# Moving the value products of a pair of query tiles behind the next scores and two sets of transposes, in the last batch and in the first batch's first two groups

## The chip, the cores and the metric

The kernel runs on one core of a Trainium2 chip, as a single launch. The metric is the time of the whole program in microseconds (us) on the device: 785.86 us for the kernel before, the median of three runs (783.3 to 787.12). A core has five engines that run their own instruction lists in order and meet at semaphores: TensorE (PE in the profile, for matrix products and for transposes through an identity matrix), VectorE (DVE), ScalarE (ACT), GpSimd (POOL) and SyncE (SP, which issues transfers).

## The reference, cut to what matters

The reference is one decoder layer on 4 batches of 512 tokens with 512 features: attention, then an expert layer, then a feed-forward layer with quantized weights. The change lies in the attention alone, which has 16 heads of 32 features, a band of keys and four sink keys:

```python
q = q.reshape(b, s, NUM_HEADS, HEAD_DIM).transpose(0, 2, 1, 3)
...
scores = jnp.einsum('bhqd,bhkd->bhqk', q, k) * scale
...
    banned = _sliding_window_banned(s, kv_len)       # (j >= SINKS) & (j < pos - WINDOW)
    scores = jnp.where(banned[None, None], -jnp.inf, scores)
probs = jax.nn.softmax(scores, axis=-1)
out = jnp.einsum('bhqk,bhkd->bhqd', probs, v)
out = out.transpose(0, 2, 1, 3).reshape(b, s, D_MODEL)
return out @ Wo.T + bo
```

A query keeps the four sink keys, all keys after it, and the 128 keys before it. Scores and projections are formed as three products of rounded halves (high by high, high by low, low by high), so that they keep nearly full precision.

## The kernel before

The attention phase takes the first 457 us of the profiled execution. It works batch by batch (`b`), in each batch by groups of four heads (`g`), and in each group by four tiles of 128 queries (`qt`). One step of this is a **unit** (g, qt). `g = 4` of a batch stands for group 0 of the next one, since the work is staged one batch ahead.

What PE does in a unit is written out by hand in `unit` of `tensor_program` and sets the order of everything: first the **scores** of the next unit (L948, and the band's mask at L956), into the PSUM tile `s_ps`; then the transposes of this unit's probabilities, slots 0 and 1 (L976, four heads each, into the two halves of `pT_ps`); then one **side** product into `side_ps` if the tables `PROJECTED` and `IN_ROUND` have one for this unit (a projection Q, K, V or O of twelve products, L889); then the slots 2 and 3. In units with qt = 2 a slot holds the sinks (L972), in those with qt = 3 slots 2 and 3 hold the sinks and the reciprocal sums `norm` (L969). At the end of the units with an odd qt comes `attend_pair`: the **value products** of the two query tiles qt - 1 and qt (L998, and L990 for the sinks) into `pv_ps`. In the first three batches the units (1, 3), (2, 0), (2, 1) and (2, 2) close with a transposition of the next batch's input, **X0** to X3 (L894), also through `side_ps`.

Round this loop three engines hand work on. DVE takes the maxima of the scores (L724), copies slots 1 and 3 out of PSUM (L745; L742 for the reciprocal sums), and multiplies the finished values with the reciprocal sums (`attn_of`, L736). ACT copies slots 0 and 2 (L560) and takes the **exponentials** of the next unit's scores (`exps`, L548), which it writes to `probs`. The next scores wait until all four exponentials of the unit before have read `s_ps`. `side_ps` is one bank: each side product waits until the one before it has been taken away, a projection K by ACT (`k_hi`, L523 and L525) and then DVE (`k_lo`, L644 and L648).

The exponentials of query tiles 0 and 1 and of tiles 2 and 3 share room: `probs` holds the pair 0, 1 in its first part and the pair 2, 3 in a part that overlaps tile 1. So the exponentials of tile 3 write where those of tile 1 were, and those of the next group's tile 1 where those of tile 3 were.

Groups 0 and 1 of the first batch and groups 1 to 3 of the last have few side products or none: `PROJECTED` names Q and K for group 1, V for group 2, and the last batch has no next one to prepare. There is also a chain of small DVE steps that routes tokens to experts; it stands between the units of the first batch (`tiles_needed` and its fellows). GpSimd (`widen`, `split`, L404 to L415) widens the reciprocal sums and splits the finished values.

Of the kernel before, what the change touches and what calls it, by code (L numbers as in the profile page):

```python
# [11 lines left out]
BATCH, SEQ, D = 4, 512, 512  # L12
# [3 lines left out]
HG = HEADS // GH  # L16
# [21 lines left out]
ROUTE_COUNTED, ROUTE_STEPS, ROUTE_DENSE = 10, 34, 42  # L38
# [21 lines left out]
def attention_phase(nc, io, x1, x2, slot_tokens, dense_tokens, sh):  # L60
# [7 lines left out]
    with ExitStack() as ctx:  # L68
# [123 lines left out]
        def width(qt):  # L192
            sink, kts, _ = blocks(qt)
            return SINKS * sink + P * len(kts)
# [21 lines left out]
        def units_before(b, g, qt):  # L216
            return b * GU + g * TT + qt
# [29 lines left out]
        def projected(b, g, qt):  # L247
            name = PROJECTED[g].split()[qt]
            return None if name == "-" or (g and not taken(b, name)) else name
# [9 lines left out]

        def in_key_order(keys):  # L260
            return keys.rearrange("p (u n) -> p u n", u=2)[:, :, SINKS:]

        def key_columns(keys, rows, g, qt):
            if qt < 2:
# [238 lines left out]
        def scalar_program(act):  # L503
# [39 lines left out]

            def exps(b, g, qt, s):
                act.wait_ge(max_ready, units_before(b, g, qt) * 2 + s + 1)
                at = BAND - width(qt) if qt >= 2 else 0
                for h in (2 * s, 2 * s + 1):
                    nc.scalar.activation(weights[qt][:, h, at:at + width(qt)], s_ps[:, h, 0:width(qt)], ACT.Exp,  # L548
                                         bias=neg_max[:, qt % 2, h:h + 1],
                                         accum_out=sums[:, g % 2, qt, h:h + 1]).then_inc(exp_done, 1)  # L550
# [57 lines left out]
        def vector_program(dve):  # L608
# [54 lines left out]
            done = [0]  # L663
# [68 lines left out]

            def attn_of(b, g):
                dve.wait_ge(slot_copied[1], copies_before(b, g, TT - 1, SLOTS - 1) + 1)
                dve.wait_ge(heads_done, b * HG + g + 1)
                nc.vector.tensor_tensor(norm[:], pv_ps[:], norm[:], ALU.mult).then_inc(attn_ready, 1)  # L736

            def copy_slot(b, g, qt, k):
# [9 lines left out]
            def unit(b, g, qt, last):  # L748
# [11 lines left out]
                if more:  # L760
                    maxima(b, *nxt, 0)
                    maxima(b, *nxt, 1)
                if qt == 0 and 0 < g < HG:
                    attn_of(b, g - 1)
                if prepare and qt in (1, 2):
                    for t in (2 * qt - 2, 2 * qt - 1):
# [1 line left out]
                if qt >= 2:  # L768
                    a, z = columns(qt, "sink")
                    dve.wait_ge(exp_done, units_before(b, g, qt) * GH + GH)  # L770
                    nc.vector.tensor_reduce(sinks[:], weights[qt][:, :, a:z].unsqueeze(3), AX.X, ALU.max).then_inc(sinks_gathered, 1)
                copy_slot(b, g, qt, 1)
                if prepare and qt in (1, 2):
                    dve.wait_ge(stats_step, coming * TT + 2 * qt)
                    for t in (2 * qt - 2, 2 * qt - 1):
                        variance_of(coming, t)
# [74 lines left out]
            weight_lo(5)  # L851
            for t in (1, 2):
                v_of(-1, t, v_banks[t], v_sb)
            for qt, route_parts in enumerate(((tiles_needed, rows_started), (slots_given,), (), (slots_addressed, experts_of_tiles))):
                unit(0, 0, qt, False)
                for part in route_parts:
                    part()
            assert done[0] == ROUTE_STEPS

            def batch(b, last):  # L860
                for g in range(1, HG if last else HG + 1):
                    for qt in range(TT):
                        unit(b, g, qt, last)
                        if (b, g, qt) == (0, 1, 2):
                            rows_given()
                        if (b, g, qt) == (0, 1, 3):
                            rows_addressed()
                            assert done[0] == ROUTE_DENSE
# [15 lines left out]
        def tensor_program(pe):  # L884
# [117 lines left out]
            def attend_pair(b, g, pair):  # L1002
                if pair == 0 and g:
                    pe.wait_ge(attn_ready, b * HG + g)
                    if g == HG:
                        pe.wait_ge(v_moved, b + 1)
                slots = [2, 1, 3, "sink"] if pair else slots_of(pair)
                for n, slot in enumerate(slots):
                    last = attend(b, g, pair, slot, n == 0, n + 1 == len(slots))
                if pair:  # L1010
                    last.then_inc(heads_done, 1)

            def o_begun(t):
                if t == 0:
# [4 lines left out]
            def unit(b, g, qt, last):  # L1019
                nxt = (g, qt + 1) if qt + 1 < TT else (g + 1, 0)  # L1020
                if not (last and nxt == (HG, 0)):
                    scores(b, *nxt)
                transpose_slot(b, g, qt, 0)
                transpose_slot(b, g, qt, 1)
                name = projected(b, g, qt)
                if name:
                    side(b, nth_in(b, g, name), name)
                if last and g == HG - 1 and qt >= 2:
                    o_begun(qt - 2)
                transpose_slot(b, g, qt, 2)  # L1030
                transpose_slot(b, g, qt, 3)
                if last and (g, qt) == (HG - 1, TT - 1):
                    o_begun(2)
                if qt % 2:
                    attend_pair(b, g, qt - 1)
                name = turned(b, g, qt)
                if name:
                    side(b, nth(b, name), name)
# [986 lines left out]
```

## Time and profile before

| what | value |
|---|---|
| median of three runs | 785.86 us (783.3 to 787.12) |
| profiled execution, its own time | 789.38 us |
| its span, first to last instruction | 787.3 us |
| mean granted PE clock | 0.983 of full |
| PE busy | 735.5 us, 93% of the span |
| DVE busy | 587.4 us, 75% |
| ACT busy | 473.1 us, 60% |
| POOL busy | 331.2 us, 42% |

Busy time is the time that an engine spent in instructions; a share near 100% means that the engine sets the pace, as long as its instructions don't wait inside. The granted clock says at which of its two levels, 1.2 or 2.4 GHz, PE ran: 1.00 is the upper, 0.50 the lower one. A row of the timeline gives the start and the duration of an instruction or of several alike in a row, and in square brackets the idle time of the engine before it and what ended it. The ends of PE's instructions are modelled.

### The profile page before, as it was taken

How to read it: one execution, taken by the hardware profiler on the slowest of the kernel's cores; microseconds unless marked ns; L12 is line 12 of the kernel's file. 1: busy time of each engine (PE TensorE's matmuls, PEld its weight loads, DVE VectorE, ACT ScalarE, POOL GpSimd, SP SyncE). 2: the span in 40 equal slices, each digit the busy share in tenths (PEclk: the TensorE clock that was granted, in tenths of full speed). 3: DMA queues.
4: the chain of work that ended last, by engine and by line, in shares of the span. 5: the costliest groups of instructions: out<-in, count | busy, mean ns of one | idle time of the engine just before them, and what ended most of it. 6: DMA issues, size and time to landing. Idle time of an engine off the chain costs nothing.

```text
span 787.3 us, 14189 instructions
## 1 busy us (share of the span) xinstructions
PE 735.5 (93%) x5167; PEld 512.7 (65%) x5184; DVE 587.4 (75%) x1099; ACT 473.1 (60%) x1028; POOL 331.2 (42%) x329
## 2 busy tenths in 40 slices
PE   5988999999999999999987989999998999999993
PEld 4866777777777776777764777888874444444441
DVE  6986866886667866766665548878888999999882
ACT  4565666766676665766666314444455787667761
POOL 2011205213242134254553544445546677777661
PEclk9998999999999999999999999999999999999997
DMA  9300012214130322314311356555430233333231
GB/s 314 115 1 27 28 40 95 92 44 151 40 107 29 108 85 77 108 31 153 129 40 55 54 198 258 182 197 201 140 126 25 54 88 87 94 95 102 73 92 42
DMA packets 55474, 78.33 MB, mean 99 GB/s; under 512 B 36335, under 2 KB 38383, under 8 KB 53680
## 3 DMA queue, kind: packets, MB, share of 16 engines
q1 hardware_dynamic: 46336, 51.99, 20.6%
q0 software_dynamic: 8784, 24.93, 9.8%
q8 instruction: 43, 0.70, 0.4%
q10 hardware_dynamic: 288, 0.52, 0.2%
q14 instruction: 23, 0.19, 0.1%
HBM read 56.92 MB, written 17.59 MB: 95 GB/s over the span
## 4 chain that ended last, share of the span: by engine, by line
PE 62%; DVE 20%; issue 8%; ACT 5%; POOL 2%; DMA 1%; another core or an unknown queue 0%; ACTq 0%; SPq 0%; POOLq 0%; DVEq 0%
PE side_ps L889 17%; PE pT_ps L976 10%; PE e_z_ps L1528 7%; PE y_ps L1528 7%; PE pv_ps L998 5%; PE s_ps L948 5%; DVE h L1784 4%; ACT hq L1739 2%; DVE neg_max L724 2%; DVE hw_max L1800 2%; DVE hq_big L1831 2%; PE s_ps L956 2%; PE pT_ps L889 1%; DVE probs L745 1%; ACT f_gate L1746 1%
## 5 line engine op out<-in xcount | busy, mean ns | idle before, releaser
L548 ACT ACTIVATE probs<-s_ps,neg_max 128x512 f32<-128x512 f32 (+2 forms) x256 | 152.5, 611 | 17.9 <-DVE neg_max L724 16.4
L724 DVE TENSOR_REDUCE neg_max<-s_ps 128x2 f32<-128x1024 f32 (+2 forms) x128 | 124.6, 1015 | 36.1 <-PE s_ps L956 35.0
L976 PE MATMUL pT_ps<-ident,probs 128*128 128x128 f32 x832 | 116.5, 282 | 7.8 <-DVE probs L745 7.0
L560 ACT ACTIVATE probs<-pT_ps 128x512 f32<-128x512 f32 x96 | 57.5, 599 | 98.7 <-PE pT_ps L976 97.3
L976 PEld LDWEIGHTS pT_ps<-ident,probs 128*128 128x128 f32 x832 | 95.1, 145 | 23.0 <-DVE probs L745 9.7
L745 DVE COPY probs<-pT_ps 128x512 f32<-128x512 f32 x112 | 76.8, 685 | 39.1 <-PE pT_ps L976 36.2
L1695 POOL TENSOR_TENSOR xg_own<-h,ln_w_sb 128x512 f32<-128x512 f32 x63 | 81.9, 1308 | 37.9 <-DVE h L1784 37.8
L889 PE MATMUL side_ps<-w_hi 128*128 128x512 f32 x172 | 71.0, 413 | 0.0
L412 POOL TENSOR_TENSOR aT_hi<-norm,one_col 128x512 fp32r<-128x512 f32 x15 | 15.6, 1041 | 126.6 <-DVE norm L736 88.4
L889 PE MATMUL side_ps<-w_hi,w_lo 128*128 128x512 f32 x172 | 67.5, 392 | 0.0
L889 PE MATMUL side_ps<-w_lo,w_hi 128*128 128x512 f32 x172 | 67.0, 390 | 0.0
L1739 ACT ACTIVATE hq<-hq_big,minus_offset 128x1024 bf16<-128x1024 f16 x30 | 32.9, 1142 | 37.3 <-DVE hq_big L1831 37.3
L998 PE MATMUL pv_ps<-probs,v_sb 128*32 128x256 f32 (+1 forms) x896 | 54.0, 378 | 1.4 <-DVE probs L745 0.9
L1905 PE MATMUL y_ps<-w_tern,hqT 128*128 128x512 bf16 x210 | 54.5, 379 | 0.7
L404 POOL TENSOR_TENSOR norm<-rinv,one_col 128x512 f32<-128x512 f32 x16 | 16.7, 1041 | 86.0 <-DVE rinv L731 86.0
L548 ACT ACTIVATION_READ_ACCUMULATOR probs<-s_ps,neg_max 128x1 f32 x256 | 52.8, 206 | 0.0
L1657 PE MATMUL e_xT_ps<-w_tern,xqT_home 128*128 128x512 bf16 x126 | 32.6, 378 | 7.3 <-DVE h L1784 6.5
L1800 DVE TENSOR_REDUCE hw_max<-xg_own 128x1 f32<-128x1024 f32 x32 | 38.7, 1209 | 0.1
L998 PEld LDWEIGHTS pv_ps<-probs,v_sb 128*32 128x32 f32 x896 | 25.7, 112 | 20.0 <-issue 8.0
L889 PEld LDWEIGHTS side_ps<-w_hi,w_lo 128*128 128x128 f32 x172 | 32.3, 188 | 7.4
L1905 PEld LDWEIGHTS y_ps<-w_tern,hqT 128*128 128x128 bf16 x224 | 21.4, 98 | 23.4
L889 PEld LDWEIGHTS side_ps<-w_hi 128*128 128x128 f32 x172 | 32.4, 188 | 5.9 <-DVE k_lo L648 0.4
(290 smaller groups left out, 1779.4 us busy)
## 6 DMA issues: line engine op xcount, KB each, us to landing
w_piece<-w_ffn SPq DMA_DIRECT2D x24, 512.0 KB
w_stage<-w_ffn SPq DMA_DIRECT2D x12, 1024.0 KB
xres<-x POOLq DMA_DIRECT2D x4, 1024.0 KB, 6.4
xn<-x SPq DMA_DIRECT2D x3, 1024.0 KB
x<-xres POOLq DMA_DIRECT2D x3, 1024.0 KB, 4.8
xn<-c SPq DMA_DIRECT2D x2, 1024.0 KB, 5.1
v_next<-c SPq DMA_DIRECT2D x2, 1024.0 KB, 7.5
xn<-x SPq DMA_DIRECT2D x4, 256.0 KB, 3.4
```

Of the source, the lines that this page charges most:

```text
L548: nc.scalar.activation(weights[qt][:, h, at:at + width(qt)], s_ps[:, h, 0:width(qt)], ACT.Exp, bias=neg_max[:, qt % 2, h:h + 1], accum_out ...
L560: nc.scalar.activation(out, turned_p, ACT.Identity).then_inc(slot_copied[0], 1)
L724: nc.vector.tensor_reduce(neg_max[:, qt % 2, 2 * s:2 * s + 2], s_ps[:, 2 * s:2 * s + 2, 0:width(qt)], AX.X, ALU.max, negate=True).then_inc ...
L745: nc.vector.tensor_copy(weights[qt][:, :, a:z], pT_ps[:, 1, :].rearrange("p (h n) -> p h n", h=GH))\
L889: last = nc.tensor.matmul(out, lt, r, start=(first and n == 0), stop=(final and n == len(terms) - 1))
L976: last = nc.tensor.transpose(pT_ps[:, k % 2, h * P:h * P + P], weights[qt][:, h, a:z], ident[:])
L998: last = nc.tensor.matmul(pv_ps[HD * h:HD * h + HD, to], v_sb[:, slot, f:f + HD], p, start=first, stop=final, tile_position=(0, HD * h))
L1528: last = nc.tensor.matmul(out, lt[:, k, :], r[:, at, :], start=(n == 0), stop=(n == 3 * DK - 1))
L1695: nc.gpsimd.tensor_tensor(hw[:, t % 2, c, :], h[:, t % 2, c, :], ln_w[:, c * CHK:c * CHK + CHK], ALU.mult)\
L1739: nc.scalar.activation(hq[:, cols], hq_code[:, cols], ACT.Identity, bias=minus_offset[:]).then_inc(hq_packed, 1)
L1800: nc.vector.tensor_reduce(hw_max[:, i, n:n + 1], flat(hw, i)[:, n * HALF:n * HALF + HALF], AX.X, ALU.max, apply_absolute_value=True).then_ ...
L1905: last = nc.tensor.matmul(sums_of(t), hqT[:, t % 2, k, :], down_w[:, k, :], start=(k == 0), stop=(k == FK - 1))
```

## The change

`values_late` names eight pairs of query tiles: in the last batch all but the last pair (groups 1 and 2 both pairs, group 3 the first), and in the first batch the second pair of group 0 and both of group 1. For these, `attend_pair` no longer stands at the end of the odd unit. It stands in the next unit, behind the next scores and behind the transposes of slots 0 and 1, ahead of the side product. `heads_done` now counts every pair. Since the exponentials write where the values' inputs lie, `exps` waits for `heads_done` in the units whose room the late pair still needs. On DVE, `attn_of` for a late second pair goes behind the copy of slot 1, and two parts of the routing chain move from behind unit (0, 3) to behind the units (1, 0) and (1, 1).

```diff
+        def values_late(b, g, pair):
+
+            return (b == BATCH - 1 and 1 <= g < HG and (g, pair) != (HG - 1, 2)) or b == 0 and (g, pair) in ((0, 2), (1, 0), (1, 2))
+
+        def values_of(b, g, pair):
+            return 2 * (b * HG + g) + (2 if pair else 1)
...
             def exps(b, g, qt, s):
                 act.wait_ge(max_ready, units_before(b, g, qt) * 2 + s + 1)
+                if s == 0 and qt == 3 and values_late(b, g, 0):
+                    act.wait_ge(heads_done, values_of(b, g, 0))
+                if s == 0 and qt == 1 and g and values_late(b, g - 1, 2):
+                    act.wait_ge(heads_done, values_of(b, g - 1, 2))
...
             def attn_of(b, g):
-                dve.wait_ge(heads_done, b * HG + g + 1)
+                dve.wait_ge(heads_done, values_of(b, g, 2))
...
-                if qt == 0 and 0 < g < HG:
+                follows_late = qt == 0 and 0 < g < HG and values_late(b, g - 1, 2)
+                if qt == 0 and 0 < g < HG and not follows_late:
                     attn_of(b, g - 1)
...
                 copy_slot(b, g, qt, 1)
+                if follows_late:
+                    attn_of(b, g - 1)
...
-            for qt, route_parts in enumerate(((tiles_needed, rows_started), (slots_given,), (), (slots_addressed, experts_of_tiles))):
+            for qt, route_parts in enumerate(((tiles_needed, rows_started), (slots_given,), (), ())):
...
+                        if (b, g, qt) == (0, 1, 0):
+                            slots_addressed()
+                        if (b, g, qt) == (0, 1, 1):
+                            experts_of_tiles()
...
             def attend_pair(b, g, pair):
-                if pair:
-                    last.then_inc(heads_done, 1)
+                last.then_inc(heads_done, 1)
...
                 transpose_slot(b, g, qt, 1)
+                if qt == 2 and values_late(b, g, 0):
+                    attend_pair(b, g, 0)
+                if qt == 0 and g and values_late(b, g - 1, 2):
+                    attend_pair(b, g - 1, 2)
...
-                if qt % 2:
+                if qt % 2 and not values_late(b, g, qt - 1):
                     attend_pair(b, g, qt - 1)
```

In the rows of order below, the number after L is the line in the kernel that the row belongs to; the change has shifted the lines, so that L998 of before is L1016, L990 is L1008, L948 is L966, L956 is L974, L976 is L994, L894 is L912 and L548 is L559.

**First batch, end of unit (1, 3), PE.** Before, the transposes of the reciprocal sums are followed by the value products of group 1's second pair (`pv_ps`), and these by the transposition X0 (`side_ps<-ident,xn`) and the scores of unit (2, 1):

```order
L969 MATMUL pT_ps<-ident,norm 128x128 [waits rinv_widened,slot_copied_dve]
L969 MATMUL pT_ps<-ident,norm 128x128 x3
L998 MATMUL pv_ps<-probs,v_sb 32x256 [waits slot_copied_act,slot_copied_dve]
L998 MATMUL pv_ps<-probs,v_sb 32x256 x3
L998 MATMUL pv_ps<-probs,v_sb 32x128 [waits slot_copied_act]
L998 MATMUL pv_ps<-probs,v_sb 32x128 x3
L998 MATMUL pv_ps<-probs,v_sb 32x256 [waits slot_copied_dve]
L998 MATMUL pv_ps<-probs,v_sb 32x256 x3
L990 MATMUL pv_ps<-sinks_T,v_sinks 128x256 [waits v_sinks_loaded,slot_copied_act]
L894 MATMUL side_ps<-ident,xn 128x128 [waits xn_ready,side_left]
L894 MATMUL side_ps<-ident,xn 128x128 x3
L948 MATMUL s_ps<-k_hi,q_hi 128x512 [waits exp_done]
```

Now X0 with its wait for `side_left` follows the transposes at once, and the products stand behind the scores and two sets of transposes of the next unit, ahead of the projection V0:

```order
L912 MATMUL side_ps<-ident,xn 128x128 [waits xn_ready,side_left]
L912 MATMUL side_ps<-ident,xn 128x128 x3
L966 MATMUL s_ps<-k_hi,q_hi 128x512 [waits exp_done]
L966 MATMUL s_ps<-k_hi,q_hi 128x512 x3
L966 MATMUL s_ps<-k_lo,q_hi 128x512 x4
L966 MATMUL s_ps<-k_hi,q_lo 128x512 x4
L974 MATMUL s_ps<-window_mask,ident_bf 128x124 x4
L994 MATMUL pT_ps<-ident,probs 128x128 [waits exp_done,slot_copied_act]
L994 MATMUL pT_ps<-ident,probs 128x128 x3
L994 MATMUL pT_ps<-ident,probs 128x128 [waits slot_copied_dve]
L994 MATMUL pT_ps<-ident,probs 128x128 x3
L1016 MATMUL pv_ps<-probs,v_sb 32x256 [waits slot_copied_act,slot_copied_dve]
```

Seven rows of products have moved past X0, the scores and eight transposes.

**Last batch, from unit (2, 1) to unit (2, 2), PE.** Before, the products of group 2's first pair stand between the last transposes of unit (2, 1) and the scores of unit (2, 3):

```order
L976 MATMUL pT_ps<-ident,probs 128x128 [waits slot_copied_dve]
L976 MATMUL pT_ps<-ident,probs 128x128 x3
L998 MATMUL pv_ps<-probs,v_sb 32x256 [waits slot_copied_act,attn_ready]
L998 MATMUL pv_ps<-probs,v_sb 32x256 x3
L998 MATMUL pv_ps<-probs,v_sb 32x256 [waits slot_copied_dve]
L998 MATMUL pv_ps<-probs,v_sb 32x256 x3
L998 MATMUL pv_ps<-probs,v_sb 32x256 [waits slot_copied_act]
L998 MATMUL pv_ps<-probs,v_sb 32x256 x3
L998 MATMUL pv_ps<-probs,v_sb 32x256 [waits slot_copied_dve]
L998 MATMUL pv_ps<-probs,v_sb 32x256 x3
L948 MATMUL s_ps<-k_hi,q_hi 128x260 [waits exp_done]
```

Now they stand between the first eight transposes of unit (2, 2) and its sinks:

```order
L966 MATMUL s_ps<-k_hi,q_hi 128x260 [waits exp_done]
L966 MATMUL s_ps<-k_hi,q_hi 128x260 x3
L966 MATMUL s_ps<-k_lo,q_hi 128x260 x4
L966 MATMUL s_ps<-k_hi,q_lo 128x260 x4
L974 MATMUL s_ps<-window_mask,ident_bf 128x128 x4
L994 MATMUL pT_ps<-ident,probs 128x128 [waits exp_done,slot_copied_act]
L994 MATMUL pT_ps<-ident,probs 128x128 x3
L994 MATMUL pT_ps<-ident,probs 128x128 [waits slot_copied_dve]
L994 MATMUL pT_ps<-ident,probs 128x128 x3
L1016 MATMUL pv_ps<-probs,v_sb 32x256 [waits slot_copied_act,attn_ready]
```

The scores have moved ahead of the sixteen products, and the transposes with them.

**The same place, ACT.** Before, the exponentials of unit (2, 3) wait for the maxima alone:

```order
L560 ACTIVATE probs<-pT_ps 128x4x128 [waits slot_transposed]
L548 ACTIVATE probs,sums<-s_ps,neg_max 128x260 [waits max_ready]
L548 ACTIVATE probs,sums<-s_ps,neg_max 128x260
L548 ACTIVATE probs,sums<-s_ps,neg_max 128x260 [waits max_ready]
L548 ACTIVATE probs,sums<-s_ps,neg_max 128x260
```

Now the first of them waits for the products too:

```order
L571 ACTIVATE probs<-pT_ps 128x4x128 [waits slot_transposed]
L559 ACTIVATE probs,sums<-s_ps,neg_max 128x260 [waits heads_done,max_ready]
L559 ACTIVATE probs,sums<-s_ps,neg_max 128x260
L559 ACTIVATE probs,sums<-s_ps,neg_max 128x260 [waits max_ready]
L559 ACTIVATE probs,sums<-s_ps,neg_max 128x260
```

Nothing has moved on ACT; one wait has been added, and there are eight such.

## Rows read from the trace of the kernel before

**Rows 1.** The page: busy us, share of the span, instructions.
```profile
PE 735.5 (93%) x5167; PEld 512.7 (65%) x5184; DVE 587.4 (75%) x1099; ACT 473.1 (60%) x1028; POOL 331.2 (42%) x329
```
**Rows 2.** Windows: length, busy us (count) of PE, PEld, DVE, ACT, POOL; clock, DMA.
```profile
90.00:120.00 30.00, 29.76 (x253) 23.12 (x252) 21.45 (x31) 20.79 (x57) 5.64 (x6) 1.00 0.19 59
...
390.00:420.00 30.00, 26.75 (x263) 19.30 (x256) 18.33 (x30) 18.32 (x55) 17.90 (x10) 0.94 0.21 72
```
**Rows 3.** Timeline of PE, first batch, units (1, 3) and (2, 0).
```profile
85.66 1.29 PE L998 MATMUL pv_ps<-probs,v_sb 128*32 128x256 f32 x24
...
87.86 0.66 PE L894 MATMUL side_ps<-ident,xn 128*128 128x128 f32 x4 [0.28 <-DVE k_lo L648]
88.44 0.51 PE L948 MATMUL s_ps<-k_hi,q_hi 32*128 32x512 f32 x4
...
89.57 1.05 PE L976 MATMUL pT_ps<-ident,probs 128*128 128x128 f32 x8
90.37 0.48 PE L889 MATMUL side_ps<-w_hi 128*128 128x512 f32 x1
```
**Rows 4.** Timeline of DVE, the same place.
```profile
87.59 0.21 DVE L648 SCALAR_TENSOR_TENSOR k_lo<-side_ps,bk_sb,k_hi 128x4 fp32r<-128x4 f32 x1
```
**Rows 5.** Timeline of PE: rows behind long idle times.
```profile
58.04 0.37 PE L972 MATMUL pT_ps<-ident,sinks 128*16 128x128 f32 x1 [2.18 <-DVE sinks L771]
...
422.47 0.27 PE L972 MATMUL pT_ps<-ident,sinks 128*16 128x128 f32 x1 [1.60 <-DVE sinks L771]
...
466.02 0.66 PE L1515 MATMUL e_xT_ps<-ident,e_xn 128*128 128x128 f32 x4 [1.66 <-DVE e_xn L1427]
```
**Rows 6.** Windows: the first of five stretches at the lower clock; columns as in Rows 2.
```profile
57.75:61.16 3.41, 2.98 (x25) 1.79 (x29) 2.20 (x6) 1.90 (x7) 0.00 (x0) 0.50 0.00 0
```
**Rows 7.** Timeline of ACT and PE, first batch, groups 0 and 1.
```profile
59.30 0.21 ACT L548 ACTIVATION_READ_ACCUMULATOR probs<-s_ps,neg_max 128x1 f32 x1
...
64.60 0.69 ACT L548 ACTIVATE probs<-s_ps,neg_max 128x512 f32<-128x512 f32 x1 [0.24 <-DVE neg_max L724]
...
72.58 0.22 ACT L548 ACTIVATION_READ_ACCUMULATOR probs<-s_ps,neg_max 128x1 f32 x1
...
74.44 0.40 PE L948 MATMUL s_ps<-k_hi,q_hi 32*128 32x260 f32 x4
```
**Rows 8.** Timeline of PE, last batch, group 2.
```profile
409.30 3.68 PE L976 MATMUL pT_ps<-ident,probs 128*128 128x128 f32 x16
412.90 2.02 PE L998 MATMUL pv_ps<-probs,v_sb 128*32 128x256 f32 x32
414.86 0.39 PE L948 MATMUL s_ps<-k_hi,q_hi 32*128 32x260 f32 x4
...
415.65 1.04 PE L976 MATMUL pT_ps<-ident,probs 128*128 128x128 f32 x8
...
418.88 0.50 PE L948 MATMUL s_ps<-k_hi,q_hi 32*128 32x512 f32 x4 [0.45 <-ACT probs L548]
...
424.02 2.36 PE L998 MATMUL pv_ps<-probs,v_sb 128*32 128x256 f32 x24
```
**Rows 9.** Timeline of ACT, last batch: last reads and first exponentials of units.
```profile
401.38 0.21 ACT L548 ACTIVATION_READ_ACCUMULATOR probs<-s_ps,neg_max 128x1 f32 x1
...
405.39 0.69 ACT L548 ACTIVATE probs<-s_ps,neg_max 128x512 f32<-128x512 f32 x1
...
413.00 0.22 ACT L548 ACTIVATION_READ_ACCUMULATOR probs<-s_ps,neg_max 128x1 f32 x1
...
416.79 0.47 ACT L548 ACTIVATE probs<-s_ps,neg_max 128x260 f32<-128x260 f32 x1
...
418.51 0.22 ACT L548 ACTIVATION_READ_ACCUMULATOR probs<-s_ps,neg_max 128x1 f32 x1
...
423.73 0.21 ACT L548 ACTIVATION_READ_ACCUMULATOR probs<-s_ps,neg_max 128x1 f32 x1
...
429.24 0.69 ACT L548 ACTIVATE probs<-s_ps,neg_max 128x512 f32<-128x512 f32 x1
```

More of the change, by code:

```diff
@@ L857, in vector_program @@
                     part()
-            assert done[0] == ROUTE_STEPS
             def batch(b, last):
@@ L863, in batch @@
                         unit(b, g, qt, last)
+                        if (b, g, qt) == (0, 1, 0):
+                            slots_addressed()
+                        if (b, g, qt) == (0, 1, 1):
+                            experts_of_tiles()
+                            assert done[0] == ROUTE_STEPS
                         if (b, g, qt) == (0, 1, 2):
```

## The prediction

> **What bounds the kernel now.** The page comes first: PE is busy for 93% of the span and no other engine for more than 75% [rows 1]. Next come the windows, since the change touches two stretches only. Between about 90 and 390 us PE is busy for 29.76 of 30.00 us, and the window shown is the first of ten that are much alike; in the window from 390 to 420 us, in the last batch, it is busy for 26.75 [rows 2]. So PE has room at both ends of the attention phase and none in between. Whatever lengthens PE's work just ahead of 90 us is carried through to the end; whatever shortens a wait in the last batch is gained in full, if nothing else ends there.
>
> In the last batch the timelines of PE and ACT show why PE waits. The next scores start only when the last exponential has read `s_ps`: it ends at 418.51 + 0.22 = 418.73 and the scores start at 418.88, 0.15 later [rows 8, 9]. A loop runs from scores over maxima to exponentials and back to scores. At the end of odd units the value products lie in this loop: the exponentials end at 413.00 + 0.22 = 413.22, but the next scores start at 414.86, behind products that began at 412.90 [rows 8, 9]. That delay of about 1.5 us is what the change can remove.
>
> **Durations.** A first pair's products hold PE for 414.86 - 412.90 = 1.96 us, a second pair's for 87.86 - 0.28 - 85.66 = 1.92 us (to the idle time that the next row shows) [rows 3, 8]. Scores with the mask take 89.57 - 88.44 = 1.13 us for tile 1 and 415.65 - 414.86 = 0.79 for tile 3; eight transposes take 90.37 - 89.57 = 0.80 [rows 3, 8]. I allow 0.1 from the last product to the exponential that now waits for it, an estimate below the 0.15 above.
>
> **What the change removes and adds, place by place.** A late pair leaves the end of its unit, so that the scores can start with the exponentials' end. But it comes back behind these scores and eight transposes, and the next exponentials now wait for it, with the rest of ACT's list behind them (the copy of slot 2). So the loop loses one delay and gains another. I follow the start of the exponentials, which is where the two meet.
>
> *Last batch, group 1 to 2.* The exponentials end at 401.38 + 0.21 = 401.59, so the scores start at 401.74; 1.13 + 0.80 + 1.92 + 0.1 later, at 405.69, the exponentials may start, against 405.39 before [rows 9]: +0.3.
>
> *Group 2, first pair.* Scores at 413.22 + 0.15 = 413.37, exponentials at 413.37 + 0.79 + 0.80 + 1.96 + 0.1 = 417.02 against 416.79 [rows 9]: +0.2, together +0.5.
>
> *Group 2, second pair.* Scores at 423.73 + 0.21 + 0.15 = 424.09, and with the shift of 0.5 at 424.6; exponentials at 424.6 + 1.13 + 0.80 + 1.92 + 0.1 = 428.55 against 429.24 [rows 9]. The gain is there because these products ran at half clock before: 24 of them took 2.36 us, and 1.29 in the first batch [rows 3, 8]. Together -0.7.
>
> *First pairs of groups 1 and 3.* In their new units PE has a side product or the first output products to do, so the exponentials' delay is covered, but PE gets the 1.96 us back. Before these pairs delayed the scores by 1.5 us or, where a side product stood ahead, by all of their time. I put 0.4 for both. **Last batch: -0.3 us.** Its bounds: -1.5, if the two other half-clock stretches there go as well, and +1.5, if the new idle time ahead of the scores brings one more.
>
> *First batch, group 0's second pair.* The exponentials end at 59.30 + 0.21 = 59.51 [rows 7], the scores can start at 59.66. From 57.75 to 61.16 PE runs at half clock, the first of five such stretches in the phase [rows 6]. Of the 1.13 us that the scores take, the 1.50 left of it do 0.75. The rest and the transposes end at 61.16 + 0.38 + 0.80 = 62.34, the products 1.92 later, and the exponentials start at 64.4 against 64.60 [rows 7]: -0.2. *Group 1's first pair.* The exponentials end at 72.58 + 0.22 = 72.80, the scores can start at 72.95 instead of 74.44 [rows 7]: -1.5. The 1.96 come back ahead of the projection Q3, where PE has no wait. **Together +0.3 us**, with bounds of -0.5 and +0.8.
>
> *Group 1's second pair.* This one decides. Before, its products run from 85.66 to 87.58, and X0 behind them waits another 0.28 until DVE has taken K3 away (`k_lo` ends at 87.59 + 0.21 = 87.80) [rows 3, 4]. This chain runs from the projection K3 over ACT to DVE and does not depend on the products. So X0 waits until 87.8 with or without them: their old place was free. The new one, between the transposes from 89.57 and the projection V0 at 90.37 [rows 3], lies at the start of the full stretch. PE is busy for nearly all of what follows, and no wait of size is left to give the time back. **+1.9 us**, at least 1.2, if the sinks' products overlap the next projection.
>
> *What the wait ahead of X0 does to the clock.* PE now idles from the last transposes to X0 for about 87.86 - 85.66 = 2.2 us less a tail of 0.1. Six rows of the trace stand behind an idle time of 1.60 us or more; 2.18 is the longest, 1.60 the shortest, and after five of these six PE falls to half clock for a stretch of 3.41 us; after the one of 1.66 at 466.02 it doesn't [rows 5, 6]. At half clock sixteen transposes took 3.68 us where two sets of eight at full clock would take 1.6 to 2.1 [rows 3, 8]. A stretch that PE fills therefore costs up to 1.7. **I take +1.5 us**, with bounds of 0 and 1.7.
>
> *The rest.* The moved routing steps and `attn_of`, which now stands behind a copy, change DVE's list, not its work. What the steps held up in their old place ends in the exponentials at 64.60 [rows 7], which the products' wait now sets; in their new places DVE has idle time, as PE's slower loop leaves it. Both at nothing; uncovered, they would cost what DVE then holds up, half a microsecond by my estimate. More changes between products in 32-column and scores in 32-row form cost little: scores start at 414.86 although the modelled end of the products is 412.90 + 2.02 = 414.92 [rows 8].
>
> The Trainium skill says in TensorEngine Tiling (Array Packing), section Tiling Modes, that a change of tiling mode drains TensorE, which speaks against the change, since each late pair has one change of mode more. At the 0.15 of a handover each, eight such drains would add an estimated 1.2 us and make the time 790.5; the row above shows no drain of that size, and the sum goes without it.
>
> **Sum:** -0.3 + 0.3 + 1.9 + 1.5 = +3.4 us. The profiled execution took 789.38 us with a span of 787.3 and would take 792.8; it lies 3.5 above the median of the three runs. Against that median, 785.86, I forecast 785.86 + 3.4 = **789.3 us**, 0.43% slower. Half a percent, 3.9 us, is about what a measurement of this kernel tells from no change.
>
> **The rivals.**
>
> 1. *No half clock behind X0.* The one exception among six speaks for it; then 789.3 - 1.5 = 787.8 us.
> 2. *Faster.* PE's work in the last batch is spread otherwise, and the half-clock stretches at both ends stay away. By the numbers above one is worth up to 1.7, of which about 1 us lies on the path, since part of each falls on waits. Without the one behind X0 and with four of the five gone: 0 + 1.9 - 4 = -2.1, so 783.8 us. It decides as soon as two are gone. Against it: the exponentials still end long after PE's last transposes, so idle times of 1.5 us and more remain, only elsewhere.
> 3. *Slower.* The added wait costs more than 0.1, or PE changes mode slowly. At 0.6 us more for each of the six pairs in the loop, it is 789.3 + 3.6 = 792.9 us. For it: ACT holds its whole list at this wait. Against it: no row has a handover over about 0.3.
> 4. *The change does nothing:* DVE reaches `k_lo` earlier, X0 runs early and the 1.9 is offset; 785.9 us. Against it: DVE and ACT were late there through their own lists, which the change leaves as they are.
>
> **How the numbers follow.** Forecast 0.40, rival 1 0.25, rival 2 0.15, rival 3 0.15, rival 4 0.05. The forecast's own range, by its bounds, is 787.3 to 791. Range: from 785.2, which leaves out about a half of rival 2, to 792.3, which leaves out about half of rival 3. Slower by over 0.5% (above 789.8): all of rival 3, four tenths of the forecast and a little of rival 1, 0.34. Faster by over 0.5% (below 781.9): only the far end of rival 2, 0.04. Within: 0.62.
>
> **What would show it.** Right, step by step: X0 in the first batch with an idle time of about 2 us ahead of it, ended by `k_lo`; V0 beginning about 1.9 us later behind X0 than before; a stretch of granted clock 0.50 that opens by about 90 us; in the last batch, scores that start 0.15 behind the exponentials' end in every unit, and first exponentials in tiles 1 and 3 that are released by PE's products and no longer by DVE. Wrong: X0 without that wait, a stretch from 90 to 390 us that has shrunk and gives the 1.9 back, or a last batch that is shorter by more than 1.5 us from its first unit to its last product.

## The result: slower by 1.3%

The changed kernel takes 795.81 us (median of four runs, 794.56 to 796.08), the kernel before on the same chip 784.58 us (four runs, 782.66 to 787.12). The ratio is 1.0133, with an interval of 1.0112 to 1.0154. The forecast was 789.3 us, with a range up to 792.3.

The profiled execution of the changed kernel takes 796.08 us, with a span of 794.3 and a mean granted clock of 0.981. PE's work is what it was, 5167 instructions. The page's line of busy times, which answers to [rows 1]:

```profile
PE 737.5 (93%) x5167; PEld 513.4 (65%) x5184; DVE 589.9 (74%) x1099; ACT 474.1 (60%) x1028; POOL 330.7 (42%) x329
```

**First batch, ahead of X0 and behind it.** The timeline of PE, which answers to [rows 3]:

```profile
89.13 1.12 PE L912 MATMUL side_ps<-ident,xn 128*128 128x128 f32 x4 [2.13 <-DVE k_lo L659]
90.17 0.80 PE L966 MATMUL s_ps<-k_hi,q_hi 32*128 32x512 f32 x4
...
92.14 1.92 PE L994 MATMUL pT_ps<-ident,probs 128*128 128x128 f32 x8
93.99 1.90 PE L1016 MATMUL pv_ps<-probs,v_sb 128*32 128x256 f32 x24
95.82 0.69 PE L1008 MATMUL pv_ps<-sinks_T,v_sinks 16*128 16x256 f32 x2
96.45 0.51 PE L907 MATMUL side_ps<-w_hi 128*128 128x512 f32 x1
```

X0 waits 2.13 us for `k_lo`, as forecast. But X0, the scores, the transposes and most of the products then run at half clock: eight transposes take 1.92 us where they took 1.05 before [rows 3]. The windows, with columns as in [rows 2], show how long that lasts, and that the window from 90 us on, full before with a clock of 1.00, is still full but has a clock of 0.91:

```profile
85.05:88.46 3.41, 1.41 (x8) 0.57 (x6) 2.20 (x5) 3.11 (x11) 0.00 (x0) 1.00 0.00 0
88.46:91.87 3.41, 2.74 (x18) 1.68 (x19) 1.90 (x7) 1.59 (x3) 0.00 (x0) 0.50 0.00 0
91.87:95.28 3.41, 3.41 (x29) 2.59 (x32) 2.95 (x3) 0.64 (x2) 0.00 (x0) 0.50 0.43 154
...
90.00:120.00 30.00, 29.76 (x238) 22.09 (x236) 17.73 (x26) 17.68 (x46) 5.48 (x5) 0.91 0.11 36
```

Two stretches of 3.41 us follow each other, not one. From X0 to V0 it takes 96.45 - 89.13 = 7.32 us; before, 90.37 - 87.86 = 2.51 [rows 3]. PE is full behind them, and nothing gives these 4.8 us back.

**Last batch.** The view of waits for ACT and then for PE, from 377 to 457 us (us in total, times, longest):

```profile
ACT probs L559 <- PE pv_ps L1016: 5.4, 3, 1.8
ACT probs L559 <- PE pv_ps L1008: 4.2, 2, 2.5
...
PE s_ps L966 <- ACT probs L559: 6.8, 7, 1.9
```

The exponentials now wait five times for value products, 9.6 us in all, and the scores seven times for exponentials, 6.8 us. In the trace of before the first wait does not exist, and the second comes once, with the 0.45 us in [rows 8]. One turn of this loop, in rows of PE and ACT:

```profile
412.56 0.59 PE L966 MATMUL s_ps<-k_hi,q_hi 32*128 32x388 f32 x4 [1.68 <-ACT probs L559]
...
419.91 1.93 PE L1016 MATMUL pv_ps<-probs,v_sb 128*32 128x256 f32 x32
...
424.06 0.50 PE L966 MATMUL s_ps<-k_hi,q_hi 32*128 32x512 f32 x4 [1.57 <-ACT probs L559]
...
421.97 0.48 ACT L559 ACTIVATE probs<-s_ps,neg_max 128x260 f32<-128x260 f32 x1 [1.79 <-PE pv_ps L1016]
```

The products end at 419.91 + 1.93 = 421.84, the exponentials start 0.13 later, and the next scores wait 1.57 us for them. The handover is as small as the forecast had it.

**Behind the attention phase.** In the feed-forward layer one DVE instruction takes 1.97 us whose fellows take 0.48 to 0.66:

```profile
604.13 1.97 DVE L1227 TENSOR_SCALAR xq_big<-f_xn,x_inv 128x512 f32<-128x512 f32 x1
```

**Where the time lies.** Four lengths can be read in every trace. A goes from the first exponential of unit (1, 0) to that of unit (2, 0) in the first batch (group 0's second pair and group 1's first are late in it); B from there to that of unit (2, 2) (group 1's second pair); C from the first exponential of unit (1, 0) in the last batch to DVE's last `attn_of`; F from the first to the ninth product `h` of the feed-forward layer. All the rest of the span differs little between kernels, save the start of A, which comes at 54.9 to 56.7 us, and the stretch between C and F, 141.9 to 143.8 us, both without a pattern that follows the edits.

| kernel (label) | A | B | C | F |
|---|---|---|---|---|
| before, first trace | 26.52 | 13.82 | 77.60 | 20.02 |
| before, second trace (e8) | 26.44 | 13.81 | 75.58 | 20.04 |
| before, one DVE wait more (e10) | 26.05 | 13.83 | 76.63 | 21.18 |
| none late (e5) | 25.99 | 13.83 | 78.38 | 21.18 |
| none late, three waits more (e9) | 25.97 | 13.82 | 78.39 | 20.03 |
| pair at X0 alone late (e12) | 28.74 | 17.40 | 76.14 | 20.05 |
| last batch alone (e2) | 27.48 | 13.85 | 78.31 | 21.17 |
| pair at X0 back (e1) | 25.56 | 13.83 | 79.50 | 21.19 |
| X0's wait filled (e3) | 27.10 | 15.86 | 78.39 | 21.18 |
| **after** | **27.80** | **18.68** | **79.43** | **21.19** |
| own room (e4) | 27.01 | 17.37 | 73.38 | 21.18 |
| own room, pair at X0 back (e6) | 29.20 | 13.81 | 73.49 | 21.19 |
| own room, last batch alone (e7) | 26.03 | 13.82 | 73.52 | 21.18 |
| the same, three waits more (e11) | 29.18 | 13.82 | 73.36 | 20.01 |

Of after against the first three rows in A, B and C (means 26.34, 13.82, 76.60) and the first two in F (20.03): 1.46 + 4.86 + 2.83 + 1.16 = 10.3 us. The timed difference is 0.0133 times 785, or 10.4 (11.2 between the medians). That the two agree so well is in part chance: with the same code there, A differs by 3.15 us between e7 and e11, and C by 2.02 between the two traces of before. The first trace of before hid a part of this: it lost 2.4 us in its third batch, between 309 and 341 us, in rows that no other trace has, which is most of the 3.5 by which its own time lies above the median.

### The profile page after: what moved, and what is told of

The parts are those of the page before. It is cut to its first block, busy times and chain, and to the rows that moved or that the text cites. A ratio compares the mean times of both kernels' runs of the same rounds, so it can differ in the third digit from the quotient of the medians.

```text
span 794.3 us, 14198 instructions
## 1 busy us (share of the span) xinstructions
PE 737.5 (93%) x5167; PEld 513.4 (65%) x5184; DVE 589.9 (74%) x1099; ACT 474.1 (60%) x1028; POOL 330.7 (42%) x329
## 4 chain that ended last, share of the span: by engine, by line
PE 62%; DVE 16%; ACT 10%; issue 8%; POOL 2%; DMA 1%; ACTq 0%; SPq 0%; POOLq 0%; DVEq 0%
PE side_ps L907 17%; PE pT_ps L994 9%; PE e_z_ps L1549 7%; PE y_ps L1549 7%; PE pv_ps L1016 6%; PE s_ps L966 5%; ACT probs L559 3%; DVE h L1805 3%; ACT sq_junk L1775 2%; ACT hq L1760 2%; ACT f_gate L1767 2%; DVE hq_big L1852 2%; PE s_ps L974 2%; DVE neg_max L735 2%; PE pT_ps L907 1%
## 5 line engine op out<-in xcount | busy, mean ns | idle before, releaser
L559 ACT ACTIVATE probs<-s_ps,neg_max 128x512 f32<-128x512 f32 (+2 forms) x256 | 152.5, 610 | 35.1 <-DVE neg_max L735 16.7
L994 PE MATMUL pT_ps<-ident,probs 128*128 128x128 f32 x832 | 115.8, 281 | 3.5 <-DVE probs L756 2.9
L994 PEld LDWEIGHTS pT_ps<-ident,probs 128*128 128x128 f32 x832 | 94.8, 144 | 18.2 <-issue 6.5
L1016 PE MATMUL pv_ps<-probs,v_sb 128*32 128x256 f32 (+1 forms) x896 | 53.0, 375 | 0.0
L559 ACT ACTIVATION_READ_ACCUMULATOR probs<-s_ps,neg_max 128x1 f32 x256 | 52.5, 205 | 0.0
L966 PE MATMUL s_ps<-k_hi,q_hi 32*128 32x512 f32 (+2 forms) x256 | 34.1, 467 | 9.0 <-ACT probs L559 9.0
L1016 PEld LDWEIGHTS pv_ps<-probs,v_sb 128*32 128x32 f32 x896 | 25.8, 112 | 17.9 <-issue 7.2
```

The costliest lines, as they stand in the source:

```text
L966: last = nc.tensor.matmul(s_ps[:, h, 0:width(qt)], q[rows, g % HG, cols], key_columns(k, rows, g % HG, qt), start=(n == 0), stop=(n == 2 a ...
L994: last = nc.tensor.transpose(pT_ps[:, k % 2, h * P:h * P + P], weights[qt][:, h, a:z], ident[:])
L1016: last = nc.tensor.matmul(pv_ps[HD * h:HD * h + HD, to], v_sb[:, slot, f:f + HD], p, start=first, stop=final, tile_position=(0, HD * h))
```

## The experiments

The ratios below are to the kernel before, run on the same chip. e1 to e8 ran on one chip, where before takes 785.31 us (e1 to e4) and 785.44 (e5 to e8), and e9 to e12 on another, where it takes 784.98; between the two, ratios are compared and not times. First the place of the products.

**e1: the pair at X0 back in its old place.**

```diff
-            return (b == BATCH - 1 and 1 <= g < HG and (g, pair) != (HG - 1, 2)) or b == 0 and (g, pair) in ((0, 2), (1, 0), (1, 2))
+            return (b == BATCH - 1 and 1 <= g < HG and (g, pair) != (HG - 1, 2)) or b == 0 and (g, pair) in ((0, 2), (1, 0))
```

> The changed kernel with one pair put back to its old place: the second pair of group 1 in the first batch, ahead of X0. Theory (places): in the profiles this pair cost 4.9 us, 1.9 for products that lost a free place and 3.0 for 6 us of half clock behind the idle time ahead of X0; so 4.9 less than the changed kernel, about 790.9 us. Rival (price per pair): each of the eight late pairs costs the same 1.3 us, by drains of PE at changes between products and transposes; then 1.3 less, about 794.5.

Measured: 789.41 us, ratio 1.0055 (1.0042 to 1.0068); B is back at 13.83 us. This pair costs the most of all parts, 6.4 us where the theory had 4.9, and the rival's equal price for each pair (794.5) falls; but 4 us of loss stay, which the terms of the theory do not hold.

**e2: only the pairs of the last batch late.**

```diff
+            return b == BATCH - 1 and 1 <= g < HG and (g, pair) != (HG - 1, 2)
```

> Late pairs in the last batch alone, none in the first. Theory (places): the last batch lost 1.8 us between the profiles, so about 786.4 us; up to 788.5 if the 2 us that the two profiles leave unexplained lie there. Rival (price per pair): five pairs at 1.3, about 791.

Measured: 789.80 us, ratio 1.0053 (1.0037 to 1.0069). e1 and e2 differ by the first batch's other two pairs and agree within 0.4 us, so no cost of those can be told. The theory's 786.4 falls; its upper end of 788.5 lies at the edge of the interval. 4 us of loss are in the last batch or in no products at all.

**e3: X0's wait filled.** The products of the pair at X0 are done twice, once in the old place, where nothing counts them, and once in the new.

```diff
+                if (b, g, qt) == (0, 1, 3):
+                    attend_pair(b, g, 2, counted=False)
```

> The changed kernel with the products of the pair ahead of X0 done twice: once in the old place, uncounted, and again in the new place, where they start afresh. The idle time ahead of X0 is filled, and PE's work grows by one pair. Theory (clock): no half clock behind X0, and 3.0 us less than the changed kernel, about 792.8. Rival (the clock has no part; only the moved work costs): the doubled work lies in the wait, so no change, 795.8; and 797.7 if it isn't free there.

Measured: 790.98 us, ratio 1.0069 (1.0052 to 1.0086): with 2 us more work on PE it is 4.8 us faster than after. By the traces 2.82 of this lie in B; A and C, with the same code there, differ by 1.7 more. The timeline of PE and a window from X0 on:

```profile
87.11 0.69 PE L1008 MATMUL pv_ps<-sinks_T,v_sinks 16*128 16x256 f32 x2
88.09 0.66 PE L912 MATMUL side_ps<-ident,xn 128*128 128x128 f32 x4 [0.28 <-DVE k_lo L659]
...
87.00:97.00 10.00, 9.72 (x84) 6.71 (x80) 6.77 (x13) 5.74 (x14) 3.04 (x3) 1.00 0.15 54
```

X0 starts when `k_lo` lets it, as without the products; the clock stays at 1.00, and B is 15.86, so that the products alone cost 15.86 - 13.82 = 2.04 us. That the wait ahead of X0 brings the half clock is shown.

**e12: the pair at X0 alone late,** with three waits added to DVE's list (they are explained at e9, to which it is compared).

```diff
+            return b == 0 and (g, pair) == (1, 2)
```

> Of the late pairs only the first batch's second pair of group 1, ahead of X0, stays late; the three satisfied waits on DVE are in. Against the run with none late and the same three waits. Theory (the products cost their time and X0's wait brings half clock for about two stretches): 1.9 + 3.0 = 4.9 us more. Rival (the prediction's terms, one stretch): 3.4 more. No half clock behind X0: 1.9 more.

Measured: 790.23 us, ratio 1.0064 (1.0040 to 1.0088), above e9 by 4.56 us in the medians and 3.5 by the ratios. The trace has one stretch at half clock behind X0, and B is 17.40, 3.58 above 13.82. Rows of PE and windows:

```profile
88.42 0.66 PE L914 MATMUL side_ps<-ident,xn 128*128 128x128 f32 x4 [2.12 <-DVE k_lo L659]
...
86.16:89.57 3.41, 1.28 (x14) 0.92 (x16) 2.18 (x7) 1.75 (x6) 0.00 (x0) 1.00 0.00 0
89.57:92.98 3.41, 3.41 (x28) 2.28 (x24) 3.10 (x4) 1.77 (x4) 0.00 (x0) 0.50 0.37 121
92.98:96.39 3.41, 3.41 (x34) 2.25 (x27) 1.23 (x2) 1.73 (x5) 0.95 (x1) 1.00 0.08 32
```

Its profile fits the prediction's terms, one stretch; its times lie between those and the theory's and do not decide. Both numbers of stretches occur. Here X0 begins 1.15 us ahead of the stretch, in e4 0.02 ahead of it, and one stretch follows; in after it begins 0.67 us inside the first, and a second follows. These are three traces; what decides between one and two is not shown. The price of the first is 3.58 - 2.04 = 1.54 us, of the second 18.68 - 17.40 = 1.28.

Next the wait of the exponentials.

**e4: own room.** `probs` gets room of its own for the pair 2, 3, so that the exponentials of tile 3 and of the next tile 1 overwrite nothing that a late pair reads, and their eight waits go. All pairs stay late.

```diff
-        probs = sb("probs", [P, 2 * GH * SEQ + GH * BAND])
+        probs = sb("probs", [P, 2 * GH * SEQ + 2 * GH * BAND])
...
-                2: probs[:, 2 * GH * (SEQ - BAND // 2):].rearrange("p (u h n) -> p u h n", u=2, h=GH)}
+                2: probs[:, 2 * GH * SEQ:].rearrange("p (u h n) -> p u h n", u=2, h=GH)}
...
-                if s == 0 and qt == 3 and values_late(b, g, 0):
-                    act.wait_ge(heads_done, values_of(b, g, 0))
-                if s == 0 and qt == 1 and g and values_late(b, g - 1, 2):
-                    act.wait_ge(heads_done, values_of(b, g - 1, 2))
```

> The changed kernel with room of its own for the probabilities of tiles 2 and 3, so that the exponentials overwrite nothing that a late pair still needs, and without their eight waits for heads_done. Theory (the added wait eats the gain): the exponentials start with the maxima again, up to 1.8 us earlier in each of the six pairs without side work; the last batch loses its 1.8 and gains some 3 more: about 791 us, most of what is left being the pair ahead of X0. Rival (price per pair): the wait is nothing, drains are, so 795.8.

Measured: 788.20 us, ratio 1.0036 (1.0023 to 1.0049), 2.8 us better than the theory had. C is 73.38, 6 us below after's.

**e7: own room, and only the last batch late** (the edits of e4 and e2).

> Own room for the pair 2, 3 and no added waits, late pairs in the last batch alone. Theory: 789.8 of the run with the last batch alone, less the 0.5 that it lost and the 4.1 that the last batch gains without waits, so 785.2 us; in its trace the exponentials of tiles 1 and 3 are released by DVE's maxima and the last batch is 3 to 5 us shorter than with the waits. Rival (the waits do not matter): 789 us or more.

Measured: 784.61 us, ratio 0.9986 (0.9973 to 1.0000), 5.2 us below e2, which has the same late pairs with the waits. The view of waits for ACT, then PE, in its last batch:

```profile
ACT probs L555 <- DVE neg_max L731: 1.7, 3, 0.7
...
PE s_ps L962 <- ACT probs L555: 1.7, 5, 0.4
```

No exponential waits for products, and the scores wait 1.7 us in place of after's 6.8. Against e5 below, which has no late pair, the same routing steps and the same long `xq_big`, e7 is 2.9 us faster: the late place is worth something, and the added wait takes more than that away. No run has the own room without late pairs, so that the room alone is worth nothing is argued and not shown.

**e6: own room, the pair at X0 back** (the edits of e4 and e1).

> The tile pair 2, 3 gets room of its own in probs, so no exponentials wait for products, and group 1's second pair of the first batch is back ahead of X0. Theory (the added wait and the X0 pair are the two costs): 789.4 of the run with the X0 pair back, less 1.7 that its last batch lost and about 4.1 that the last batch gains without the waits, so 783.6 us. Rival (half-clock stretches or work behind the attention phase swallow the gain): 787 us or more.

Measured: 784.82 us, ratio 0.9998 (0.9985 to 1.0011), between theory and rival, and as e7 although two pairs of the first batch are late as well. So once more no worth of those two can be told.

Last, what lies behind the attention phase.

**e8: the kernel before, unchanged, a second trace.**

> The kernel before, unchanged, for a second trace. Theory (the 2.4 us that DVE and PE lose near 311 us in the first trace of before are no property of the kernel): no such row in this trace, 785.0 to 786.6 us, and an attention phase that ends 2 to 4 us earlier than in the first trace. Rival (they are): 788 us or more, with the same rows.

Measured: 784.95 us, a single run, with a span of 782.9. Neither the rows near 311 us nor the loss are there, and the time is near the timed median of 785.44. The attention phase, to the start of DVE's last `attn_of`, ends 5.7 us earlier than in the first trace, more than the theory's 2 to 4, since C too is 2.0 us shorter.

**e5: none late.** `values_late` returns False; the count of every pair and the routing steps' new places stay.

```diff
+            return False
```

> No pair is late; the count of every pair and the new places of the two routing steps stay. Theory (those parts cost nothing, the lost time is in the products' places and the clock): 785.3 us, the median of before on this chip, within 1 us. Rival (the routing steps' new places, or the other layout, carry part of the loss, as the 4 us that the last batch alone had lost would suggest): 788 us or more, with a DVE row behind the attention phase that is 1.5 us longer than in before.

Measured: 787.49 us, ratio 1.0031 (1.0015 to 1.0046). The rival holds in kind, at 0.5 us less than its 788: a fifth of the loss is there without a late pair. `xq_big` takes 1.95 us, as (within 0.02) in each of the kernels so far with the change's DVE list and in neither trace of before. DVE's list has one instruction more: a routing step in its new place makes a wait an instruction of its own. Counting DVE's records in the trace from 0, the first `h` behind `mean_rstd` is number 830 in before and 831 in the others, and there an idle time of 0.24 us stands ahead of it that nothing in the profile ends.

**e10 and e9: only the place in DVE's list.** e10 is the kernel before with one wait more that was satisfied long ago; e9 is e5 with three (`qt in (0, 1, 2)`).

```diff
+                if (b, g) == (2, 1) and qt in (0,):
+                    dve.wait_ge(heads_done, 1)
```

> The kernel before with one long satisfied wait added to DVE's list in the third batch, and nothing else. Theory (the position in DVE's list decides): the third xq_big from 585 us on takes 1.95 us where before has 0.48, and the time is 786.9, 1.5 us more than before. Rival (the change's routing steps decide): 0.48 and 785.4.

> No late pair, as in the run with none late, and three waits that were long satisfied are added to DVE's list in the third batch. Theory (in every kernel with the change's DVE list, one instruction longer than before, an issue gap of 0.24 us falls on a hidden-layer product near 590 us, POOL then holds the port when xq_big comes, and xq_big takes 1.95 instead of 0.48 us; three instructions more move the gap under a wait of 1.4 us): xq_big back at 0.48 and 1.5 us gone, 786.0. Rival (the routing steps' new places cause it, or it is chance): 787.5 and 1.95 again.

Measured: e10 786.81 us, ratio 1.0021 (1.0007 to 1.0035); e9 785.67 us, ratio 1.0020 (1.0003 to 1.0037). One satisfied wait makes before 1.8 us slower (1.6 by the ratio), and `xq_big` takes 1.95 us. With three waits e9's trace has 0.48 again and an F 1.15 us below e5's. Its times do not show that gain: its ratio is 0.0011 (0.9 us) below e5's, with intervals that overlap, since four of its twelve runs take 788.4 to 788.6 us and the others 784.9 to 786.3. Timeline of DVE and POOL in e8, the kernel before:

```profile
588.98 0.74 DVE L1784 SCALAR_TENSOR_TENSOR h<-up_ps,gu_scale,f_gate 128x512 f32<-128x512 f32 x1
...
593.43 0.75 DVE L1784 SCALAR_TENSOR_TENSOR h<-up_ps,gu_scale,f_gate 128x512 f32<-128x512 f32 x1 [0.72 <-PE up_ps L1657]
594.10 0.48 DVE L1206 TENSOR_SCALAR xq_big<-f_xn,x_inv 128x512 f32<-128x512 f32 x1
...
591.73 3.98 POOL L1695 TENSOR_TENSOR xg_own<-h,ln_w_sb 128x512 f32<-128x512 f32 x3
```

And in e10:

```profile
589.33 0.75 DVE L1786 SCALAR_TENSOR_TENSOR h<-up_ps,gu_scale,f_gate 128x512 f32<-128x512 f32 x1 [0.24 <-issue]
...
593.44 0.75 DVE L1786 SCALAR_TENSOR_TENSOR h<-up_ps,gu_scale,f_gate 128x512 f32<-128x512 f32 x1 [0.71 <-PE up_ps L1659]
594.11 1.95 DVE L1208 TENSOR_SCALAR xq_big<-f_xn,x_inv 128x512 f32<-128x512 f32 x1
...
592.04 3.73 POOL L1697 TENSOR_TENSOR xg_own<-h,ln_w_sb 128x512 f32<-128x512 f32 x3
```

With the gap POOL's three products start 0.3 us later. In e8 the third of them must still wait for the `h` of 593.43 (3.98 us for three), and `xq_big` goes ahead of it; in e10 it runs on without a break (3.73), to 592.04 + 3.73 = 595.77, and `xq_big` ends 0.29 later. The Trainium skill says in SBUF — State Buffer, section SBUF: two separate sides, that VectorE, where its operation needs the port pair that it shares with GpSimd, and GpSimd lock that pair exclusively, and that the loser waits out the other's instruction; these rows agree, though no run here shows that `xq_big` needs the pair. What makes the gap of 0.24 us stays open: the runs tie it to the place in DVE's list and to nothing else. The Trainium skill says in Runtime: NRT & Kernel Launch, section Instruction fetch mechanics, that lists are fetched in blocks at a cost that is mostly hidden; no run here shows whether this gap is one.

**e11: own room, only the last batch late, and the three waits** (the edits of e7 and e9).

> Own room for the pair 2, 3, late pairs in the last batch alone, and the three satisfied waits on DVE. Theory: 784.6 of the run without the three waits less 1.5, so 783.1 us, faster than before by about 0.3%. Rival: 784.6, no gain from the place of the gap.

Measured: 782.78 us, ratio 0.9968 (0.9951 to 0.9985), the one version whose interval lies clear below the kernel before. F is back at 20.01. Against e7, on the other chip, the ratio is 0.0018 (1.4 us) lower with intervals that overlap, so the theory's 1.5 us for the waits fits but is not shown by the times.

## Why the prediction was wrong, step by step

*X0's wait and the old place.* Right: the idle time ahead of X0 is 2.13 us, ended by `k_lo`, and the products' old place was free. *Group 1's second pair, +1.9.* Right: 2.04 (e3).

*Half clock behind X0, +1.5 with a bound of 1.7.* The price of a stretch was right, 1.54 and 1.28, but the bound was not: it supposed that one idle time brings one stretch. In after there are two, 2.82 us together. Rival 1, none at all, never came in the three traces that have this idle time. But an idle time of that size does not always bring half clock: the one of 2.18 us in [rows 5] stands in all 14 traces (2.17 or 2.18), and half clock is there or opens within 2.5 us behind it in five. The rule of five in six came from one trace.

*Group 0's second pair and group 1's first, +0.3.* Not refuted: e1 against e2 and e6 against e7 differ by 0.4 us at most, with both signs, and each of the four has an interval of about 1 us either way. The 1.46 us that A has in after's trace is no price of these pairs, since A is 25.56 in e1 with the same code up to there; where the half-clock stretches of A fall differs from trace to trace.

*Last batch, -0.3 with bounds of -1.5 and +1.5.* This step failed. Six traces without late pairs in the last batch have a C of 75.58 to 78.39 (mean 77.12), four with late pairs and waits 78.31 to 79.50 (mean 78.91): +1.8, and +2.3 against the three traces with before's place for all products (76.60). The times of e2 against e5, which differ by these five pairs alone, give +2.3 (1.7 by the ratios). The handover was not at fault, at 0.13 us for an assumed 0.1. Nor was the loop's arithmetic: from the first exponential of unit (2, 1) to that of (2, 3), traces without half clock there have 10.97 us early (e8) and 11.20 late (e2, e3), the forecast's +0.2.

The term that failed is the -1.2 for group 2's second pair: it took half clock in that place as gone with the products. From unit (2, 3) to (3, 1) the first trace of before has 12.45 us, with a stretch at half clock, so that 11.25 were forecast; the four late kernels have 12.80 to 12.88, each with such a stretch. That is 1.6 us. Without the stretch the early place has 10.88 to 10.91 (e8, e10, e12). In after, rows of PE and a window:

```profile
427.65 0.27 PE L990 MATMUL pT_ps<-ident,sinks 128*16 128x128 f32 x1 [1.60 <-DVE sinks L783]
...
429.79:433.20 3.41, 3.41 (x28) 2.31 (x24) 2.50 (x3) 0.60 (x1) 0.00 (x0) 0.50 0.02 5
```

This idle time ahead of the sinks is the 1.60 us at 422.47 in [rows 5]. It stands in all 14 traces, and the change does not touch it. A stretch at half clock opens within 2.2 us behind it in three of the six traces without late pairs in the last batch and in all eight with them, the four with own room among them, where no wait of the scores for exponentials is over 0.4 us. So the new idle times of 1.6 to 1.9 us ahead of the scores are not needed for it; whether the late place makes it more frequent is not shown. The first pairs and the step from group 1 to 2 cost a little more than was put: +0.55 us to unit (2, 1) and +0.47 from unit (3, 1) on, 1.0 for an assumed 0.7.

*The rest at nothing.* This failed too. The routing steps' move added one instruction to DVE's list, and one instruction more costs 1.16 us in the traces (F) and 1.6 to 1.8 us timed (e10). No row of the attention phase could have shown it.

*The baseline.* The trace of before that the sum was made against lost 2.4 us in its third batch and had three half-clock stretches in the last; the step for the last batch was made on rows that a typical run does not have, C 77.60 where the second trace has 75.58.

Together the errors of the sum are 1.3 for the second stretch, 2.1 to 2.6 for the last batch and 1.2 to 1.8 for the rest (DVE's list); with the forecast's 3.4 that makes 8.0 to 9.1 of the 10.4 us. By the traces what is left lies in A; its cause stays open, since whether after's runs have two stretches there each time, as its trace does from 57.74 to 64.56 us, was not settled.

## What to carry to other kernels

A step that is taken out of a loop and put back in front of the loop's next stage gains here only where the next stage need not wait for it: room of its own for the operands (e7 against e2, 5.2 us) was worth more than the new place (e7 against e5, 2.9 us). A term that rests on half clock going away needs the idle time ahead of it to go away too; here that idle time belonged to another wait. An old place that lies under a wait is free twice, in time and as work that keeps the clock up, so price both before leaving it. And before a difference of 0.2% is put down to an edit, move the instruction list of the other engines by a few satisfied waits and see if it stays.

## What the runs showed of the hardware that was not expected

One idle time of 2.13 us on PE was followed by two stretches of 3.41 us at half clock, though PE was busy for all of the second and for 2.74 us of the first; idle times of 2.12 us in e4 and e12 were followed by one. One satisfied wait more in DVE's list, at 271.65 us and so 317 us earlier in the program, made the kernel before 1.8 us slower; 1.14 us of it lie in F, by way of a gap of 0.24 us, a change of order between POOL and DVE, and an `xq_big` of 1.95 us in place of 0.48.
